# Extra products of a matrix of ones inside the attention of a fused decoder layer

## What is computed

```python
x = x + _L0_attn_ref(_layernorm(x), W_in, conv_w, dt_bias, A_log, D, norm_w, W_out)   # a state-space mixer
x = x + _L0_xattn_ref(_layernorm(x), ctx_512, ctx_512)                                # cross attention
x = x + _L0_ffn_ref(_layernorm(x), router_logits, gating_einsum, linear, per_expert_scale, router_scale)  # 8 experts, top 2
...
scores = jnp.einsum('bkgsd,bktd->bkgst', qh, kh) * scale     # 8 batches, 256 tokens, 32 query heads, 8 key heads of 16
attn = jax.nn.softmax(scores, axis=-1)
out = jnp.einsum('bkgst,bktd->bkgsd', attn, vh)
```

## Time and profile before

| | |
|---|---|
| runs | 1459.42 us median of 3 (1452.49 to 1459.96) |
| profiled execution | 1459.7 us, span 1457.9 us |
| TensorE busy over the span | 1343.5 us (92%) |
| VectorE, ScalarE, GpSimd busy | 877.1, 723.6 and 586.2 us |
| mean granted TensorE clock | 0.954 |
| attention | 703 to 982 us |

### The profile page before, as it was taken

The page is one execution under the profiler, slowest core; times in us unless marked ns, Lnnn a source line. Parts: engine busy times, 40 slices in busy tenths (PEclk is TensorE's granted clock), DMA queues, the critical chain, the costliest instruction groups (busy, mean ns, idle before and its releaser), DMA issues.

```text
span 1457.9 us, 23107 instructions
## 1 busy us (share of the span) xinstructions
PE 1343.5 (92%) x7729; PEld 734.2 (50%) x7729; DVE 877.1 (60%) x1838; ACT 723.6 (50%) x1390; POOL 586.2 (40%) x871
## 2 busy tenths in 40 slices
PE   6699999999999999998888888888999999999997
PEld 4456566666666665654333433323444444444443
DVE  5797898979797979757888888855111111111111
ACT  2676667667666676663576776762111111111110
POOL 1365465555455465675223245243222222222221
PEclk9899999999999999997898997988999999999999
DMA  9000000000000000000211110002443354244322
GB/s 338 10 8 5 8 5 1 12 1 12 1 8 5 8 6 8 13 1 5 97 34 34 34 34 31 30 30 74 121 134 114 66 138 135 46 130 132 58 44 29
DMA packets 40291, 73.00 MB, mean 50 GB/s; under 512 B 18544, under 2 KB 22896, under 8 KB 39152
## 3 DMA queue, kind: packets, MB, share of 16 engines
q1 hardware_dynamic: 30240, 48.10, 9.5%
q0 software_dynamic: 8736, 20.61, 7.6%
q10 hardware_dynamic: 1200, 2.82, 0.5%
HBM read 148.91 MB, written 19.99 MB: 116 GB/s over the span
## 4 chain that ended last, share of the span: by engine, by line
PE 68%; DVE 21%; issue 5%; ACT 3%; POOL 2%; DMA 1%; SPq 1%; POOLq 0%; DVEq 0%; ACTq 0%
PE work_ps L539 12%; PE gate_ps L1530 9%; PE up_ps L1530 9%; PE down_ps L1514 9%; PE work_ps L611 7%; DVE conv L820 7%; PE work_ps L544 4%; DVE maxes L1220 3%; PE work_ps L633 3%; PE work_ps L1046 3%; PE mturn_ps L544 2%; PE decay_ps L1037 2%; DVE mix L736 2%; PE decay_ps L621 2%; PE work_ps L1022 1%
## 5 line engine op out<-in xcount | busy, mean ns | idle before, releaser
L539 PE MATMUL work_ps<-xnT,w_in 128*128 128x256 f32 (+1 forms) x1216 | 299.8, 391 | 2.8 <-DVE xdt L860 2.1
L736 POOL TENSOR_TENSOR mix<-decay,cbm 128x512 f32<-128x512 f32 x128 | 182.9, 1431 | 221.6 <-ACT decay L731 190.6
L539 PEld LDWEIGHTS work_ps<-xnT,w_in 128*128 128x128 f32 (+1 forms) x1216 | 219.2, 188 | 65.1 <-issue 33.4
L727 ACT ACTIVATE decay<-decay_ps 128x512 f32<-128x512 f32 x256 | 154.3, 603 | 111.6 <-PE decay_ps L621 111.0
L1618 POOL DMA_INDIRECT out_dram<-y_out,ids x39 | 61.9, 1587 | 334.3 <-DVE row_w L1582 228.9
L1220 DVE TENSOR_REDUCE maxes<-work_ps 128x2 f32<-128x512 f32 x256 | 166.6, 683 | 33.7 <-PE work_ps L1022 32.1
L820 DVE SCALAR_TENSOR_TENSOR conv<-raw,conv_w,conv 128x256 f32<-128x256 f32 x240 | 177.7, 746 | 6.6 <-ACT conv L687 0.7
L1118 ACT ACTIVATE prob<-decay_ps 128x512 f32<-128x512 f32 x256 | 142.2, 609 | 75.3 <-PE decay_ps L1037 74.4
L1597 DVE TENSOR_TENSOR act<-gelu,up_ps 128x512 f32<-128x512 f32 x39 | 26.8, 688 | 252.1 <-PE up_ps L1530 252.1
L731 ACT ACTIVATE decay<-decay 128x512 f32<-128x512 f32 x256 | 163.9, 640 | 4.7 <-PE work_ps L539 3.0
L1530 PE MATMUL gate_ps<-w_e,xgT 128*128 x312 | 140.5, 593 | 1.4 <-ACT xgT L1547 1.0
(11 more groups left out here) (270 smaller groups left out, 1975.8 us busy)
## 6 DMA issues: line engine op xcount, KB each, us to landing
w_e<-c_experts_dram SPq DMA_DIRECT2D x39, 3072.0 KB
normed_tokens<-r_xn SPq DMA_DIRECT2D x17, 256.0 KB, 2.1
out_dram<-x_sb SPq DMA_DIRECT2D x17, 256.0 KB, 2.5
x_sb<-x_dram SPq DMA_DIRECT2D x1, 3072.0 KB, 16.8
w_in<-c_w_inT_dram ACTq DMA_DIRECT2D x1, 2560.0 KB, 12.7
w_in<-c_w_inT_dram SPq DMA_DIRECT2D x1, 2048.0 KB, 9.1
w_out<-c_w_outT_dram SPq DMA_DIRECT2D x1, 2048.0 KB, 21.9
RT<-cum_scratch SPq DMA_DIRECT2D x32, 48.0 KB
```

The costliest lines, as they stand in the source:

```text
L539: m = e.matmul(ps[0:width, at:at + L], w_in[:, k, col:col + width], xnT[b % 2][:, k, :], start=(k == 0), stop=(k == KD - 1))
L727: e.activation(decay[s % 5][:, :], decay_ps[s % 3][:, :], ACT.Relu, scale=-1.0).then_inc(piece_done[stage], 1)
L736: return e.tensor_tensor(four(mix[s % 5]), four(decay[s % 5]), cb, ALU.mult)
```

## The change

A new piece `warm` with a slot number `nxt` and a count. TensorE waits for `exponent` of item nxt-3 (what the `score` of item nxt waits for too) and issues `count` products of ones into `score_ps[nxt % 3]`, the bank that this score then overwrites. Other engines do nothing for it. There are 150 such products:

- two behind each `product` of batches 1 to 6 (48 groups, 96 in all);
- five ahead of `n_turn` of the first half for batches 2 to 7, in slot 13 of batches 1 to 6 (30);
- ten between the first `c_rank` and `c_count` in batch 4 (10);
- one in every second slot of batch 7, from slot 4 on (14).

`repeated` gets the bank as an argument; its old uses keep `score_ps[2]`.

```diff
+                put(i, ("warm", i + 1, 2))            # behind ("product", i - 3), n <= i < n * (NB - 1)
...
-            put(n * (b - 1) + n // 2 * (h + 1) - LEAD + 2, ("n_turn", b, h))
+            at = n * (b - 1) + n // 2 * (h + 1) - LEAD + 2
+            if b > 1 and h == 0:
+                put(at, ("warm", at + 1, 5))
+            put(at, ("n_turn", b, h))
...
-        put(at + 3, ("c_rank", g), ("c_count", g))
+        put(at + 3, ("c_rank", g), *[("warm", at + 4, 10) for _ in range(g == 0)], ("c_count", g))
...
+    for i in range(n * (NB - 1) + 4, n * NB - 1, 2):
+        put(i, ("warm", i + 1, 1))
...
-        def repeated(e, count):
+        def repeated(e, bank, count):
 
             many = m_ones[:, :].rearrange("p (o j) -> p o j", o=1).to_broadcast([P, 4, P])
             for _ in range(count):
-                e.matmul(score_ps[2][:, :], m_ones[:, :], many, start=True, stop=True)
+                e.matmul(bank[:, :], m_ones[:, :], many, start=True, stop=True)
...
+            elif stage == "warm":
+                nxt, count = key
+                e.wait_ge(*done("r_init"))
+                e.wait_ge(*done("exponent", nxt - 3))
+                repeated(e, score_ps[nxt % 3], count)
```

More of the change, by code:

```diff
@@ L172, in mixer_slots @@
     return slots
-DMA_ONLY = {"freed", "mixed", "cum_out", "cum_in", "ctx_in", "n_out", "router_in", "first_expert", "r_store", "out_in", "c_weight_out", "keep_warm"}
+DMA_ONLY = {"freed", "mixed", "cum_out", "cum_in", "ctx_in", "n_out", "router_in", "first_expert", "r_store", "out_in", "c_weight_out", "keep_warm", "warm"}
 def bank_use(stage, *key):
@@ L229, in attention_slots @@
             put(i, ("product", i - 3))
+            if n <= i < n * (NB - 1):
+                put(i, ("warm", i + 1, 2))
     for b in range(NB):
@@ L997, in tensor_attention @@
                 e.wait_ge(*done("exponent", NB * N_ITEMS - 1))
-                repeated(e, key[1])
-            if stage == "mixed":
+                repeated(e, score_ps[2], key[1])
+            elif stage == "warm":
[3 more added lines that the diff above has]
+                repeated(e, score_ps[nxt % 3], count)
+            elif stage == "mixed":
                 e.wait_ge(*done("x_add", NT - 1))
@@ L1515, in down @@
                 m.then_inc(downed, 1)
-            repeated(e, 14)
+            repeated(e, score_ps[2], 14)
             turn_x(0)
-            repeated(e, 3)
+            repeated(e, score_ps[2], 3)
             for i in range(MT):
```

## The result

The changed kernel takes 1468.99 us (median of 10 runs, 1462.29 to 1471.45), the kernel before 1457.31 (10 runs beside it, 1452.49 to 1459.96): a ratio of 1.0069, 95% interval 1.0050 to 1.0088, some 10 us. (The ratios of this document are estimated from all the runs of both kernels and are not the quotients of the medians.) 1457.4 had been forecast, no change that can be told; the forecast's own range ended at 1464, that with the rivals at 1470, and slower had 0.24.

A forecast was written before the change was run, and what follows sets the result against it. TensorE, busy 92% of the span, was taken as bound in the router stretch, VectorE in others. 4.9 + 0.5 - 3.8 + 0.4 + 0.3 = 2.3 us gain from 1459.7 gave 1457.4 us; range 1452 to 1464, with rivals 1446 to 1470.

The forecast's parts named there:

- Quarters 0 and 3: First and last eight items of a batch; nine at full clock to lose 3.8 us, bounds 0 to 7.6.
- Quarter 1: Second eight items of batches 1 to 6: clock regained gains 4.9 us, limited by VectorE's idle time; bounds 0 to 12.9.
- Quarter 2: Third eight items of a batch, with router transposes and logits, TensorE the bound: 11.5 us long, 0.5 us gained in all.
- Quarter 2 of batch 6: Third eight items of batch 6, without cold time: to lose 0.8 us to its pairs.
- Even batches: First eight items of batches 2 and 4, VectorE's alone: 0; last eight of batch 4: 0.4 us gained.
- Batch 7: Fourteen single ones cost 0.8 and 0.6 us, the last eight items regain 1.7: 0.3 us gained in all.
- The ones hold the clock: Batches 1 to 6: ones in waits and slots remove nearly all of some 52 us cold time; clock 0.97 or more.
- The third rival: Batches 1 to 6 and 7: the ones don't hold the clock, its gains fall away; slower, 1469 us, chance 0.09.
- The first rival: Clock pays in full, TensorE pacing second eight items behind the wait: 10.4 us for 4.9; faster, 1448 us, chance 0.33.
- The ones on the path everywhere: Ones delay the next score and maxima throughout batches 1 to 7, no slack takes them; slower, 1470 us, chance 0.15.
- about 12 us of ones on the path: Closing remark on the attention's sum: this cost of ones set against 14 us of clock regained.

## Why the prediction was wrong

It had the trade right, clock regained against ones on the path, and missed both sizes. Step by step:

- **Quarters 0 and 3: the step that failed.** I took the first pair as hidden and the second as on the path, 0.42 us a quarter and 3.8 in all. Measured are 0.9 in quarter 0, 0.75 in quarter 3 and 1.1 in both of batch 6, 7.9 in all, at and over the bound of 7.6 that I had set aside. Two things were wrong. The first pair isn't hidden: ScalarE's slack takes most of it, but the maxima stand behind it too, and VectorE already waited for them. This had been named as a bound and not counted. In quarter 3 the first pair costs 0.2 us, with VectorE's wait up from 0.15 to 0.61, and the pairs behind score and maxima give 2.2 of 3.1 us back in batch 1. And the second pair holds the score up by 0.54 us, not 0.42.
- **Quarter 1: mis-sized.** The clock came back in full, and the gain was 0.9 us for 4.9. Without pairs and cold time the quarter takes 10.1 us in batch 1, and VectorE idles for only 0.2 of it. The bound was VectorE, as I said, but I took its busy time of before, 9.55 us in 25 instructions, as fixed. With the clock up 27 instructions and 9.92 us fall within the quarter, and less in the next (7.81 us for 8.34). The pairs then add 0.4 to 0.5, which I had put into a slack that isn't there.
- **Quarter 2: right in batches 1, 2, 3, 5.** 11.7 us for the forecast 11.5, from 10.7 without pairs, as read off the slope of before.
- **Quarter 2 of batch 6: a wait not seen.** I gave it 0.8 us for its pairs. The four us came with the clock, down for 6.8 us, half of that right behind a wait for the router's rows. This wait grows where TensorE arrives sooner. It is not the pairs' doing, since it is there without them, and 2.31 us long with no ones at all.
- **Even batches.** I gave quarter 0 of batches 2 and 4 nothing, as VectorE's alone, cold or not; together they are 1.5 us shorter. Quarter 3 of batch 4 was to gain 0.4 and is 0.9 longer; no run takes that term apart.
- **Batch 7**: +0.3 us forecast, 0.5 measured, which is luck in part. The single ones cost 1.2 us in quarters 0 to 2, not 0.8, and the last quarter, warm throughout, is 1.7 shorter. By my terms it would have been 2.7 if it stayed warm (3.3 less 0.6).
- **The ones hold the clock**: right; cold time went from some 52 to 10 us. The third rival is out.
- **The first rival** is out as well: with the clock up quarter 1 gives some 0.5 us for its 3.4 us of cold time in batch 1, VectorE pacing the rest. The Trainium skill ("TensorE: Matmul & The Clock Gate", Terms) has throttled time cost itself times one minus the granted ratio; by it the 42 us of cold time gone are an estimated 21 us. The trace agrees in quarter 2 (1.7 us for 3.4) and not in quarter 1.
- **The ones on the path everywhere** was the rival that came true in the main, nearly with its time (1470), at a chance of 0.15. The experiment with four ones shows it in batch 1. In the first halves of the even batches it doesn't hold: the pairs are free there.
- **A remark that doesn't fit its terms**: "about 12 us of ones on the path" against 14 regained. The terms add up to some 10 against 12; the sum of 2.3 us stands.

The time stayed within the wide range, not within the forecast's own one; the way it moved was missed.

## What to carry to other kernels

Work that only keeps a clock up was free in a wait of its engine and in stretches that another engine fills, and cost its full time elsewhere: place it where the engine stands, not at regular spacing, and never ahead of what two other engines wait for. In batch 1 a pair ahead of a score cost 0.39 us on average (3.1 us for eight), behind it 0.11. Before paying for a clock, ask which engine paces the cold stretch: where TensorE did (quarter 2) half of the cold time came back, behind a full VectorE (quarter 1) some 0.5 us of 3.4. And follow the order on: when one wait is filled, the next engine's lateness becomes the next wait.

## What the runs showed of the hardware

- A product of ones is 0.21 us behind another one, but a pair between f32 products and a 49-row score takes 0.54: the score starts 0.31 us behind the second of them.
- TensorE was at 1.2 GHz for 12 us in the router's stretch of batch 6 (13.40 us, clock 0.55), in the kernel with ones in the waits only, though the profile has it busy for 13.17 of the 13.40. Busy time by the profile doesn't tell whether the clock stays up.
- Many falls came behind waits of 1.2 to 2.3 us, but a wait neither suffices nor is needed. In quarter 1 of batch 6 TensorE waited for the maxima for 1.29 us in the kernel before and 3.4 us of cold time followed; in the kernel with no ones it waited for 1.30 us and none did. And quarter 2 of batch 6 had 3.4 us of cold time in one kernel with no wait over 0.34 us in it or just ahead of it. The same code showed quarter 2 of batch 3 at 10.7 us and full clock in one kernel and at 13.1 us and 0.74 in another.
- The granted clock rose from 0.954 to 0.976 over the span while the time rose by 0.7%: it is no measure of a gain.
